# Attention 1 of a four-part layer stack: the causal mask applied to the probabilities by GpSimd instead of to the scores by TensorE

## The chip, the cores and the metric

The kernel runs on one core of a Trainium2 chip. The metric is the device time of one execution in microseconds (us); the median of three runs before the change is 2347.13 us, with 2340.8 and 2350.67 us as the lowest and the highest.

## The reference

A sequence of 2 x 1024 tokens of width 128 goes through four layers: a hybrid attention with a state-space branch (attention 0, not causal), a mixture of experts, a latent attention (attention 1, causal), and a second mixture of experts. The change touches attention 1 alone:

```python
q_lat = einsum('bhtd,hdl->bhtl', q, k_eff)
attn = einsum('bhtl,bsl->bhts', q_lat, c_kv) / sqrt(hs)
attn = where(triu(ones((T, T), bool), k=1), -inf, attn)
attn = softmax(attn, axis=-1)
ctx = einsum('bhts,bsl->bhtl', attn, c_kv)
```

A query at position t must get nothing from keys behind it: their scores are minus infinity, so their probabilities are zero. There are 16 heads of width 8.

## The kernel before

`attention` (line 276) is called for both attentions; only the call of `latent_attention` (line 1877) is causal. It works in `UNITS` = 8 units, one for each group of four heads and each half of the batch. A unit has two passes that are interleaved on the engines.

The **max pass** computes scores with the queries on the partitions (`max_unit`, line 469: a score product of each 512 keys, then on the diagonal tile a product of the identity with `mask_qk` that adds -1e30 where the key lies behind the query). VectorE takes the maximum of each row (`take_max`, line 677), splits the negated maxima into three bf16 parts (`combine`, line 683), TensorE turns them (`turn_max`), ScalarE copies them to `mrow` (`rows`, line 610), and SyncE sends them by DMA into rows 96 to 98 of `qa` (`rows`, line 412), so that the second score product subtracts the maximum.

The **exp pass** has the keys on the partitions. It goes through `NE` = 24 slots (`exp_units`, line 321): 8 for the first 512 queries (query block 0, key tiles 0 to 3, two pairs of heads each) and 16 for the second 512 (key tiles 0 to 7). `MID` = 8 is the first slot of query block 1. In a slot `exp_unit` (line 501) computes the scores of two heads, `c0` being the first query that a key tile reaches, so a slot on the diagonal is 512, 384, 256 or 128 queries wide. Where key tile and query block meet on the diagonal (`kt // 4 == qb`: slots 0 to 7 and 16 to 23), each of the two products is followed by a second one of the identity with `mask_kq` (line 517). ScalarE takes the exponential of each head into one of four buffers `probs` (line 630, f32). `pv_quad` (line 521) multiplies the probabilities of two neighbouring slots with the values; it is done in two parts, in odd slot s for slots s-3 and s-2.

What sets the order: each engine runs its own list, in order, and waits on semaphores. TensorE's list is `body` (line 560): in slot s first, if s is odd, part 0 of the product with the values, then score products of the max pass that a planner has put there in proportion to their columns (`places`, lines 336 to 347), then `exp_unit(s)`, more of the max pass, then part 1. `exp_unit` waits until ScalarE has emptied the score bank (slot s-1); ScalarE waits until the values' product of slot s-4 is done. SyncE's list (lines 438 to 445) puts, for unit i, the copies `mirror(i+1)`, then the 18 loads of unit i+2 (`load`, allowed once all scores of unit i-1 are done, that is at the start of unit i), then `rows(i, 1)`, whose arrival `exp_unit` awaits at slot `MID`, then `rows(i+1, 0)`. The last two units have no loads to make. GpSimd does nothing in these 8 units: its list (line 448) holds the preparation only, with the casts of `ident_b`, `mask_kq` and `mask_qk` (lines 453 to 456) and clearing of `ka`.

The two lines of the products with the values that matter here:

```python
if part == 0:
    pe.wait_ge(probs_ready, 2 * (NE * i + kt_slot + 2))
```

Of the kernel before, what the change touches and what calls it, by code (L numbers as in the profile page):

```python
# [6 lines left out]
BF16 = mybir.dt.bfloat16  # L7
I32 = mybir.dt.int32
ALU = mybir.AluOpType
# [6 lines left out]
BLK = 512  # L16
NBLK = T // BLK
TILE = 128
# [108 lines left out]
def sl(i, w=BLK):  # L127
    return slice(i * w, (i + 1) * w)
# [147 lines left out]
def attention(k, tag, q_lin, k_lin, k_heads, v_aug, causal, attn_t, front=None):  # L276
# [5 lines left out]
    nc = k.nc  # L282
# [5 lines left out]
    KROWS = MROW + 3  # L288
    QT = SEQ // TILE
    UNITS = 2 * GROUPS  # L290
    CONSTS = 3 if causal else 1
    RING = 3
    with ExitStack() as ctx:
        qa = [k.sb(f"{tag}_qa{i}", [KROWS, 4, SEQ], BF16, ctx) for i in range(RING)]
        ka = [k.sb(f"{tag}_ka{i}", [KROWS, nk, SEQ], BF16, ctx) for i in range(RING)]
        qu = [k.sb(f"{tag}_qu{i}", [128, 4, SEQ], BF16, ctx) for i in range(2)]
        ku = [k.sb(f"{tag}_ku{i}", [128, nk, BLK], BF16, ctx) for i in range(2)]
        probs = [k.sb(f"{tag}_probs{i}", [128, 2, BLK], F32, ctx) for i in range(4)]
# [6 lines left out]
        rden = k.sb(f"{tag}_rden", [128, 4, 4], F32, ctx)  # L305
        attn_tok = k.sb(f"{tag}_tok", [128, NT, HEADS * HD], F32, ctx)
        ident_b = k.sb(f"{tag}_identb", [128, 128], BF16, ctx)
        mask_kq = k.sb(f"{tag}_maskkq", [128, 128], BF16, ctx)
        mask_qk = k.sb(f"{tag}_maskqk", [128, 128], BF16, ctx)
        scores_max = [p.rearrange("p h t -> p (h t)") for p in k.pair[0:2]]  # L310
        scores_exp = [k.bank[4], k.bank[5]]
# [9 lines left out]
        exp_units = []  # L321
        for qb in range(2):
            for kt in range(QT if not causal else 4 * (qb + 1)):
                c0 = max(0, kt * TILE - qb * BLK) if causal else 0
                for hp in range(2):
                    exp_units.append((qb, kt, hp, c0))
        NM, NE = len(max_units), len(exp_units)
        half_end = [max(s for s, u in enumerate(exp_units) if u[0] == qb) for qb in range(2)]


# [3 lines left out]
        MID = half_end[0] + 1  # L334
        DUE = MID - 6 if not causal else MID - 5
        cost = [n + 70 for _, _, n in max_units]
        own_from = min(n for n in range(NM + 1) if sum(cost[n:]) * NE <= sum(cost) * (DUE + 1))
        stream = [(0, n) for n in range(own_from, NM)] + [(1, n) for n in range(own_from)]
        places, done, spent = [], 0, 0
        for place in range(2 * NE):  # L340
# [5 lines left out]
            done = upto  # L346
# [11 lines left out]
        const_ready = k.sem(f"{tag}_const")  # L358
# [7 lines left out]
        mrow_sent = [k.sem(f"{tag}_mrow_sent{h}") for h in range(2)]  # L366
        exp_scored = k.sem(f"{tag}_exp_scored")
        probs_ready = k.sem(f"{tag}_probs_ready")
        pv_done = k.sem(f"{tag}_pv_done")
        osb_ready = k.sem(f"{tag}_osb_ready")  # L370
        oturned = k.sem(f"{tag}_oturned")
# [16 lines left out]
        with nc.Block() as block:  # L388
# [58 lines left out]
            @block.gpsimd  # L447
            def _(pool):
                nc.gpsimd.memset(ka[0][64:96, :, :], 0.0).then_inc(k_cleared[0], 1)
                pool.wait_ge(k_cleared[0], 2)  # L450
                if front:
                    front.gpsimd_first(pool)
                nc.gpsimd.tensor_copy(ident_b[:, :], k.m("ident")).then_inc(const_ready, 1)
                if causal:
                    nc.gpsimd.tensor_copy(mask_kq[:, :], k.m("mask_kq")).then_inc(const_ready, 1)
                    nc.gpsimd.tensor_copy(mask_qk[:, :], k.m("mask_qk")).then_inc(const_ready, 1)
                pool.wait_ge(const_ready, CONSTS)
                for i in range(1, RING):
                    nc.gpsimd.memset(ka[i][64:96, :, :], 0.0).then_inc(k_cleared[i], 1)
                    pool.wait_ge(k_cleared[i], 2)  # L460
                if front:
                    front.gpsimd_second(pool)

            @block.tensor
            def _(pe):
                def kj(j):
                    return 0 if shared else j
# [33 lines left out]
                def exp_unit(i, s):  # L501
                    qb, kt, hp, c0 = exp_units[s]
                    if s == 0:
                        pe.wait_ge(mrow_sent[0], 48 * (i + 1))
                    if s == MID:
                        pe.wait_ge(mrow_sent[1], 48 * (i + 1))
                    for jj in range(2):
                        if i > 0 or s > 0:
                            pe.wait_ge(probs_ready, 2 * (NE * i + s) + jj - 1)
                        j = 2 * hp + jj  # L510
                        out = scores_exp[jj]
                        diag = causal and kt // 4 == qb
                        ins = nc.tensor.matmul(out[:, c0:BLK], ka[i % RING][:, kj(j), sl(kt, TILE)],  # L513
                                               qa[i % RING][:, j, qb * BLK + c0:(qb + 1) * BLK], start=True,
                                               stop=not diag)
                        if diag:
                            ins = nc.tensor.matmul(out[:, c0:c0 + TILE], ident_b[:, :], mask_kq[:, :],
                                                   start=False, stop=True)
                        ins.then_inc(exp_scored, 1)

                def pv_quad(i, kt_slot, vstage, part):

                    qb, kt, _, c0 = exp_units[kt_slot]
                    if part == 0:
                        pe.wait_ge(probs_ready, 2 * (NE * i + kt_slot + 2))
                        if kt_slot == 0:
                            pe.wait_ge(vstaged, i + 1)
                        if kt_slot == 0 or kt_slot == MID:
                            pe.wait_ge(osb_ready, 2 * i + qb)
                    mid = (c0 + BLK) // 2  # L530
                    cols = slice(c0, mid) if part == 0 else slice(mid, BLK)
                    for j in range(4):
                        last = nc.tensor.matmul(out_acc[32 * j:32 * j + 32, cols], vstage[:, kt, kj(j), :],  # L533
                                                probs[(kt_slot + j // 2) % 4][:, j % 2, cols],

                                                start=kt == 0 and part == 0,
                                                stop=kt_slot + 1 == half_end[qb], skip_group_check=True)
                    if part == 1:
                        last.then_inc(pv_done, 2)
# [20 lines left out]
                def body(i):  # L560
                    for s in range(NE):
                        odd = s % 2 == 1
                        if odd and s > 1:
                            products_with_v = (i, s - 3, vst[i % 2])
                        elif odd and i > 0:
                            products_with_v = (i - 1, NE - 2, vst[1 - i % 2])
                        else:
                            products_with_v = None
                        if products_with_v:
                            pv_quad(*products_with_v, 0)  # L570
                        first_pass(i, 2 * s)
                        exp_unit(i, s)
                        if s == done_half[1] + 2:
                            turn_max(i, 1)
                        if s == done_half[0] + 2 and i + 1 < UNITS:
                            turn_max(i + 1, 0)
                        first_pass(i, 2 * s + 1)
                        if products_with_v:
                            pv_quad(*products_with_v, 1)
                        if s == 3 and i > 0:  # L580
                            turn_out(i - 1, 1)
                        if s == MID + 3:
                            turn_out(i, 0)

                if front:
                    front.tensor_first(pe)
                pe.wait_ge(const_ready, CONSTS)
                for n in range(own_from):
# [7 lines left out]
                for part in range(2):  # L596
                    pv_quad(UNITS - 1, NE - 2, vst[1], part)
# [617 lines left out]
def hybrid_attention(k, d, x_in, consts_in, rest_in, hc, rall, attn_t):  # L1215

    with ExitStack() as ctx:
        v_aug = k.sb("v_aug", [128, NT, KV, 32], ctx=ctx)
        work = [buf[:, sl(b)] for buf in (attn_t, k.hn) for b in blocks(T)]
        work += [k.sb(f"front_work{i}", [128, BLK], ctx=ctx)[:, :] for i in range(2)]  # L1220
        front = HybridFront(k, d, ctx, x_in, consts_in, rest_in, hc, rall, v_aug, work)
        attention(k, "attn0", by_head(d["q_lin"]), by_head(d["k_lin"][:, 0:32]), KV, v_aug, False, attn_t, front)
# [603 lines left out]
def latent_attention(k, d):  # L1826

    nc = k.nc
    with ExitStack() as ctx:
# [12 lines left out]
        with ExitStack() as pre:  # L1842
# [32 lines left out]
            split3(k, "split_q1", [(qf, parts, tmp, send_linear(k, d["q_lin"], parts))], T)  # L1875
            split3(k, "split_k1", [(kf, parts, tmp, send_linear(k, d["k_lin"], parts))], T)
        attention(k, "attn1", by_head(d["q_lin"]), by_head(d["k_lin"]), HEADS, v_aug, True, attn_t)
        with nc.Block() as block:
            @block.vector
# [691 lines left out]
```

## Time and profile before

| What | Value |
|---|---|
| median of 3 runs | 2347.13 us |
| the profiled execution's own time | 2365.25 us |
| its span in the profile | 2363.4 us |
| TensorE busy, share of the span | 1855.2 us, 78% |
| VectorE busy | 1590.9 us, 67% |
| ScalarE busy | 1403.2 us, 59% |
| GpSimd busy | 647.2 us, 27% |
| mean granted TensorE clock | 0.836 of full speed |

Line numbers (L517) are those of the kernel before. "banks" are the PSUM banks; attn_probs, attn_qa, attn_ka, attn_mrow are the buffers named above. PE is TensorE, PEld its weight load, DVE VectorE, ACT ScalarE, POOL GpSimd, SPq the queue of SyncE. A matmul's end is modelled, so distances from one start to the next say more than durations. "[x <-y]" in a timeline is the engine's idle time before the instruction and what ended it. An f32 product with the values stands in the timeline as two instructions for each of the four heads (x8).

### The profile page before, as it was taken

To read this page: it belongs to the slowest core of one execution; us is meant where nothing else is said; L and a number is where in the kernel's file an instruction comes from. 1 tells how busy PE (TensorE), PEld (TensorE's weight loads), DVE (VectorE), ACT (ScalarE), POOL (GpSimd) and SP (SyncE) were. 2 spreads that over 40 slices of the span, in tenths; PEclk is the share of its full clock that TensorE was granted. 3 is DMA by queue.
4 is the path that set the end of the run, shared out by engine and by line. 5 is a ranking of instruction groups with operands and counts; after the bars stand their busy time and mean duration, and the time that the engine had idled before them with its cause. 6 is when DMAs were issued, how large, how long until landed. Compare 5 with 4: busy or idle time off the path is not lost. (4 is left out here: it accounts for less than half of the span.)

```text
span 2363.4 us, 31926 instructions
## 1 busy us (share of the span) xinstructions
PE 1855.2 (78%) x10382; PEld 767.3 (32%) x10382; DVE 1590.9 (67%) x1569; ACT 1403.2 (59%) x2909; POOL 647.2 (27%) x347
## 2 busy tenths in 40 slices
PE   6899999963766666776776778739998995999994
PEld 1233333322333332333333433413333334333331
DVE  6788888533999998899999231366555533466463
ACT  2477777724999996999998122305555462453432
POOL 1000000000888888788888001010000000000000
PEclk8799999986788877777767779659898896799996
DMA  3211210002655553665554010043222100000000
GB/s 141 53 24 27 43 26 12 2 0 63 214 205 195 194 191 122 206 211 189 194 194 143 1 72 0 29 96 52 35 48 44 27 2 15 0 0 0 0 5 13
DMA packets 56819, 182.31 MB, mean 77 GB/s; under 512 B 8357, under 2 KB 11712, under 8 KB 55040
## 3 DMA queue, kind: packets, MB, share of 16 engines
q1 hardware_dynamic: 56056, 179.74, 24.9%
q10 hardware_dynamic: 648, 1.04, 0.2%
q8 instruction: 71, 1.16, 0.2%
q14 instruction: 44, 0.36, 0.1%
HBM read 160.56 MB, written 7.21 MB: 71 GB/s over the span
## 5 line engine op out<-in xcount | busy, mean ns | idle before, releaser
L1585 POOL TENSOR_TENSOR hc<-st,ct 128x1024 f32<-128x1024 f32 x256 | 599.2, 2361 | 102.5 <-DVE st L1564 102.5
L680 DVE TENSOR_REDUCE attn_mx<-banks 128x1 f32<-128x1024 f32 (+7 forms) x512 | 502.2, 990 | 177.8 <-PE banks L485 120.9
L630 ACT ACTIVATE attn_probs<-banks 128x512 f32<-128x512 f32 (+3 forms) x896 | 446.2, 550 | 278.1 <-PE banks L513 177.6
L1564 DVE TENSOR_TENSOR_SCAN st<-da,banks 128x1024 f32<-128x1024 f32 x256 | 568.6, 2271 | 28.6 <-ACT da L1525 21.6
L1533 ACT ACTIVATE ut<-b_turned,x_now 128x128 f32<-128x128 f32 x1280 | 389.4, 387 | 1.7
L1453 PE MATMUL banks<-mats,ut 128*128 128x128 f32 x1280 | 251.4, 344 | 96.7 <-DVE st L1564 74.6
L1525 ACT ACTIVATE da<-dt,a_now 128x1024 f32<-128x1024 f32 x256 | 286.9, 1139 | 21.5 <-DVE st L1564 13.5
L513 PE MATMUL banks<-attn_qa,attn_ka 99*128 99x512 bf16 (+3 forms) x896 | 274.6, 376 | 19.8 <-DMA attn_qa<-attn_mrow 17.9
L533 PE MATMUL banks<-attn_probs,attn_vst 128*32 128x256 f32 (+3 forms) x3584 | 273.7, 377 | 4.1 <-ACT attn_osb L621 3.8
L1453 PEld LDWEIGHTS banks<-mats,ut 128*128 128x128 f32 x1280 | 190.4, 169 | 234.3 <-ACT ut L1533 144.7
L483 PE MATMUL banks<-attn_ka,attn_qa 64*128 64x512 bf16 (+3 forms) x512 | 203.1, 397 | 74.0 <-DMA attn_ku<-attn_ka 52.2
L1469 PE MATMUL banks<-hc,onecol 128*32 128x512 f32 x1024 | 189.1, 822 | 65.9 <-POOL onecol L1583 53.0
L2167 PE MATMUL banks<-hid_m,ew 128*128 128x512 f32 x320 | 150.2, 613 | 0.0
L483 PE MATMUL banks<-attn_ku,attn_qu 64*128 64x512 bf16 (+3 forms) x384 | 145.7, 380 | 0.0
L513 PEld LDWEIGHTS banks<-attn_qa,attn_ka 99*128 99x128 bf16 x896 | 80.9, 98 | 146.9 <-ACT attn_probs L630 55.3
L483 PEld LDWEIGHTS banks<-attn_ka,attn_qa 64*128 64x128 bf16 x512 | 47.9, 94 | 246.6 <-issue 174.4
L1460 PE MATMUL banks<-xparts,sel 96*128 96x512 bf16 x192 | 73.1, 470 | 57.4 <-DVE st L1564 56.8
L1279 POOL MEMSET onehot<- 128x1024 bf16 x1 | 1.0, 956 | 421.9 <-SPq L1265 421.9
L1558 DVE TENSOR_TENSOR banks<-bt,banks 128x1024 f32<-128x1024 f32 x96 | 115.9, 1207 | 0.0
L533 PEld LDWEIGHTS banks<-attn_probs,attn_vst 128*32 128x32 f32 x3584 | 73.7, 109 | 102.9 <-issue 91.9
L2343 DVE TENSOR_TENSOR beta<-beta,beta_raw 128x1536 f32<-128x1536 f32 x8 | 14.1, 1758 | 106.0 <-ACT beta L2273 106.0
L2167 PEld LDWEIGHTS banks<-hid_m,ew 128*128 128x128 f32 x320 | 58.3, 192 | 70.5 <-issue 70.5
(409 smaller groups left out, 1829.4 us busy)
## 6 DMA issues: line engine op xcount, KB each, us to landing
dt<-dt_rows SPq DMA_DIRECT2D x256, 512.0 KB, 4.1
attn_qa<-q_lin SPq DMA_DIRECT2D x144, 64.0 KB
attn_qu<-attn_qa SPq DMA_DIRECT2D x16, 512.0 KB, 4.2
moe_w<-in_moe_w SPq DMA_DIRECT2D x2, 2048.0 KB, 9.9
attn_ka<-k_lin SPq DMA_DIRECT2D x63, 64.0 KB
mats<-in_mats SPq DMA_DIRECT2D x1, 2844.5 KB, 15.1
attn_ku<-attn_ka SPq DMA_DIRECT2D x8, 256.0 KB, 5.0
q_lin<-qparts SPq DMA_DIRECT2D x6, 256.0 KB
```

Of the source, the lines that this page charges most:

```text
L483: ins = nc.tensor.matmul(out[:, lo:hi], lhs, rhs, start=True, stop=not diag)
L513: ins = nc.tensor.matmul(out[:, c0:BLK], ka[i % RING][:, kj(j), sl(kt, TILE)], qa[i % RING][:, j, qb * BLK + c0:(qb + 1) * BLK], start=Tru ...
L533: last = nc.tensor.matmul(out_acc[32 * j:32 * j + 32, cols], vstage[:, kt, kj(j), :], probs[(kt_slot + j // 2) % 4][:, j % 2, cols],  star ...
L630: nc.scalar.activation(probs[s % 4][:, jj, c0:BLK], scores_exp[jj][:, c0:BLK], ACT.Exp, scale=scale).then_inc(probs_ready, 1)
L680: nc.vector.reduce_max(mx[:, qt, j:j + 1], scores_max[n % 2][:, 0:w], AX.X)\
L1453: ins = nc.tensor.transpose(pair[:, i // 4, sl(i % 4, TILE)], buf[:, i, :], k.m("ident"))
L1469: last = nc.tensor.matmul(y_bank[h][32 * g:32 * g + 32, :], col[jp % 2][:, :], hc[(4 * jp + g) % 8][:, sl(h)], start=False, stop=False, sk ...
L1525: nc.scalar.activation(da[n % 4][:, :], dt[n % 4][:, :], ACT.Exp, scale=a_now[:, g, jp:jp + 1])\
L1533: nc.scalar.activation(ut[TURNED.index(n) % 2][:, i, :], b_turned[:, 8 * b + i, :], ACT.Copy, scale=x_now[:, i, g, jp:jp + 1]).then_inc(ut ...
L1564: nc.vector.tensor_tensor_scan(st[n % 4][:, :], da[n % 4][:, :], pair[:, :, :].rearrange("p h t -> p (h t)"), 0.0, ALU.mult, ALU.add).then ...
L1585: nc.gpsimd.tensor_tensor(hc[n % 8][:, :], st[n % 4][:, :], ct[:, b * SEQ:(b + 1) * SEQ], ALU.mult)\
L2167: last = nc.tensor.matmul(out[:, :], w2[:, p, comp * D:(comp + 1) * D], hid_m[u % 2][:, s, p, :], start=False, stop=p == PAIRS - 1)
```

## The change

GpSimd gets a loop. For each of the 16 diagonal slots of a unit it waits until both exponentials of the slot are written, and sets to zero, in place, every element of the 128 x 2 x 128 diagonal tile whose key (partition) lies behind its query (column), by position. TensorE's product of identity and `mask_kq` falls away, as do `mask_kq` and its cast. Part 0 of the products with the values waits in addition for both selects of its two slots. The mask of the max pass stays.

```diff
-    CONSTS = 3 if causal else 1
+    CONSTS = 2 if causal else 1
...
-        mask_kq = k.sb(f"{tag}_maskkq", [128, 128], BF16, ctx)
...
+        DIAGONAL = [s for s, (qb, kt, _, _) in enumerate(exp_units) if causal and kt // 4 == qb]
...
+        probs_cut = k.sem(f"{tag}_probs_cut")
...
-                    nc.gpsimd.tensor_copy(mask_kq[:, :], k.m("mask_kq")).then_inc(const_ready, 1)
...
+                def cut(i, s):
+
+                    _, _, _, c0 = exp_units[s]
+                    done = len(DIAGONAL) * i + DIAGONAL.index(s)
+                    pool.wait_ge(probs_ready, 2 * (NE * i + s + 1))
+                    if done:
+                        pool.wait_ge(probs_cut, done)
+                    own_keys = probs[s % 4][:, :, c0:c0 + TILE]
+                    nc.gpsimd.affine_select(out=own_keys, in_=own_keys, compare_op=ALU.is_ge, fill=0.0, base=0,
+                                            pattern=[[0, 2], [1, TILE]], channel_multiplier=-1).then_inc(probs_cut, 1)
+
+                for i in range(UNITS):
+                    for s in DIAGONAL:
+                        cut(i, s)
...
-                        diag = causal and kt // 4 == qb
-                        ins = nc.tensor.matmul(out[:, c0:BLK], ka[i % RING][:, kj(j), sl(kt, TILE)],
-                                               qa[i % RING][:, j, qb * BLK + c0:(qb + 1) * BLK], start=True,
-                                               stop=not diag)
-                        if diag:
-                            ins = nc.tensor.matmul(out[:, c0:c0 + TILE], ident_b[:, :], mask_kq[:, :],
-                                                   start=False, stop=True)
-                        ins.then_inc(exp_scored, 1)
+                        nc.tensor.matmul(out[:, c0:BLK], ka[i % RING][:, kj(j), sl(kt, TILE)],
+                                         qa[i % RING][:, j, qb * BLK + c0:(qb + 1) * BLK], start=True,
+                                         stop=True).then_inc(exp_scored, 1)
...
                         pe.wait_ge(probs_ready, 2 * (NE * i + kt_slot + 2))
+                        if kt_slot in DIAGONAL:
+                            pe.wait_ge(probs_cut, len(DIAGONAL) * i + DIAGONAL.index(kt_slot) + 2)
```

## Rows read from the trace of the kernel before

**Rows 1.** Busy time by stretch: halves of units 4, 6, 7; sum of all 16 halves.

```profile
core 0: us, PE busy (x) PEld busy (x) DVE busy (x) ACT busy (x) POOL busy (x), PEclk, DMA share, GB/s
...
1774.17:1793.85 19.68, 14.33 (x141) 7.08 (x142) 10.63 (x23) 7.93 (x20) 0.00 (x0) 0.92 0.46 62
1793.85:1824.51 30.66, 30.61 (x235) 11.05 (x236) 16.26 (x24) 15.71 (x34) 0.00 (x0) 0.78 0.13 27
...
1873.68:1889.00 15.32, 14.16 (x141) 7.06 (x142) 10.08 (x22) 7.93 (x20) 0.00 (x0) 1.00 0.01 2
1889.00:1914.08 25.08, 24.96 (x238) 9.72 (x238) 16.73 (x25) 15.61 (x34) 0.00 (x0) 1.00 0.01 2
...
1926.22:1948.38 22.16, 21.48 (x200) 7.68 (x200) 0.55 (x2) 15.21 (x33) 0.00 (x0) 0.85 0.00 1
sum 353.98, PE 327.81 PEld 133.58 DVE 194.52 ACT 187.28 POOL 0.00; mean PE 20.49 PEld 8.35 DVE 12.16 ACT 11.71 POOL 0.00
```

**Rows 2.** Waits, 1590 to 1950 us: who waited for whom, total, times, longest.

```profile
PE banks L513 <- DMA attn_qa<-attn_mrow: 16.9, 7, 4.2
```

**Rows 3.** Timeline of PE: a slot with masks, then one without (start, us).

```profile
1862.63 0.39 PE L513 MATMUL banks<-attn_qa,attn_ka 99*128 99x512 bf16 x1
...
1862.85 0.22 PE L517 MATMUL banks<-attn_maskkq,attn_identb 128*128 128x128 bf16 x1
...
1862.91 0.38 PE L513 MATMUL banks<-attn_qa,attn_ka 99*128 99x512 bf16 x1
...
1863.28 0.39 PE L483 MATMUL banks<-attn_ka,attn_qa 64*128 64x512 bf16 x1
...
1899.84 0.60 PE L513 MATMUL banks<-attn_qa,attn_ka 99*128 99x512 bf16 x2
...
1900.38 0.39 PE L483 MATMUL banks<-attn_ka,attn_qa 64*128 64x512 bf16 x1
```

**Rows 4.** SyncE's timeline: the first load of unit 7, at unit 5's start.

```profile
1824.14 0.27 SPq L385 DMA_DIRECT2D attn_ka<-k_lin  x1
```

**Rows 5.** Groups of GpSimd instructions: shapes, count | busy, mean ns.

```profile
L1281 POOL TENSOR_SCALAR_AFFINE_SELECT onehot<-onehot 128x1024 bf16<-128x1024 bf16 x1 | 3.0, 3013 | 0.2 <-POOL onehot L1279 0.2
...
L889 POOL TENSOR_TENSOR hn<-attn_t,qparts 128x512 f32<-128x512 f32 x2 | 2.3, 1154 | 39.0 <-ACT qparts L1052 39.0
...
L1583 POOL CAST onecol<-onehot 128x32 f32<-128x32 bf16 x8 | 1.7, 207 | 47.5 <-POOLq L238 40.7 <-POOLq L1593 6.7
...
L453 POOL CAST attn_identb<-mats 128x128 bf16<-128x128 f32 x2 | 0.6, 290 | 3.9 <-DVE attn_ka L727 3.2 <-DMA cols<-in_cols 0.7
```

**Rows 6.** Timeline: GpSimd starts after a VectorE instruction that it awaits.

```profile
1551.41 3.47 DVE L727 MEMSET attn_ka<- 3x4096 bf16 x1 [0.91 <-issue]
...
1554.94 3.50 POOL L459 MEMSET attn_ka<- 32x4096 bf16 x1 [2.29 <-DVE attn_ka L727]
```

**Rows 7.** Timeline, units 5 and 6: second exponentials and the products that use them.

```profile
1864.88 1.09 ACT L630 ACTIVATE attn_probs<-banks 128x512 f32<-128x512 f32 x2 [0.62 <-PE banks L517]
...
1867.07 0.64 PE L533 MATMUL banks<-attn_probs,attn_vst 128*32 128x256 f32 x8
...
1868.13 0.87 ACT L630 ACTIVATE attn_probs<-banks 128x384 f32<-128x384 f32 x2 [0.73 <-PE banks L517]
...
1869.68 0.53 PE L533 MATMUL banks<-attn_probs,attn_vst 128*32 128x192 f32 x8
...
1870.96 0.66 ACT L630 ACTIVATE attn_probs<-banks 128x256 f32<-128x256 f32 x2 [0.62 <-PE banks L517]
...
1872.14 0.42 PE L533 MATMUL banks<-attn_probs,attn_vst 128*32 128x128 f32 x8
...
1873.26 0.45 ACT L630 ACTIVATE attn_probs<-banks 128x128 f32<-128x128 f32 x2 [0.63 <-PE banks L517]
...
1874.81 0.32 PE L533 MATMUL banks<-attn_probs,attn_vst 128*32 128x64 f32 x8
...
1875.61 1.08 ACT L630 ACTIVATE attn_probs<-banks 128x512 f32<-128x512 f32 x2 [0.30 <-PE banks L517]
...
1877.33 0.64 PE L533 MATMUL banks<-attn_probs,attn_vst 128*32 128x256 f32 x8 [0.19 <-ACT attn_osb L621]
```

**Rows 8.** Timeline, unit 7, slots 16 to 19: the same for the last unit.

```profile
1939.86 2.31 ACT L630 ACTIVATE attn_probs<-banks 128x512 f32<-128x512 f32 x4 [0.35 <-PE banks L517]
...
1942.55 0.64 PE L533 MATMUL banks<-attn_probs,attn_vst 128*32 128x256 f32 x8
```

## The prediction

> **What bounds the kernel now.** I read the busy time by stretch first, cutting the 8 units of attention 1 at slot 0 and at slot MID, then the waits, then the timelines of a few slots. The 16 halves cover 353.98 us of the span, TensorE is busy for 327.81 us of them, ScalarE for 187.28 and GpSimd for none [rows 1]. Everything that the change does happens in these 354 us.
>
> Two different things set the end there.
>
> The second half of a unit (slots 8 to 23) is TensorE's. At full clock it takes 25.08 us with TensorE busy for 24.96 [rows 1], and the starts in a slot follow each other without a hole: score products, max pass, values, score products again. Whatever is taken off TensorE's list here comes off the time, and whatever makes it wait is added.
>
> The first half (slots 0 to 7) of units 1 to 5 is the DMA's. In unit 6, which has no loads beside it, it takes 15.32 us; in unit 4, with the same instructions and 14.33 us of TensorE work, 19.68 us [rows 1]. The rest is a pause before slot MID for the row maxima, up to 4.2 us and seven times in all [rows 2]. The maxima lie in SyncE's queue behind 18 loads that start with the unit (1824.14 us for unit 5, which began at 1823.8) [rows 4], and no speed of TensorE in slots 0 to 7 brings their landing forward. So what is gained in the first half of units 1 to 5 becomes a longer pause. The same holds for unit 0, where the loads are issued before the unit starts (its pause is under half a microsecond). Behind each long pause the granted clock is at its lower level (1.2 GHz) for a while: the second half of unit 4 ran at 0.78 and took 30.66 us, that of unit 6 at 1.00 and took 25.08 [rows 1]. A drop costs up to 5.6 us.
>
> **Part 1: 256 mask products go.** In a slot with masks the score products start at 1862.63 and the next line at 1863.28, 0.65 us; without masks 1899.84 to 1900.38, 0.54 us [rows 3]. The mask starts at 1862.85 and the next score product 0.06 us later. So a mask costs 0.055 us of TensorE's list, not the 0.22 us that its row shows, and a slot 0.11 us. Eight diagonal slots in each half: 0.9 us off each half at full clock (they lie in slots 16 to 23, which the timelines show at full clock). ScalarE starts 0.05 us sooner after the first score product, the product with the values 0.11 us sooner per slot.
>
> The cast of mask_kq (about 0.29 us, as the 128x128 cast in [rows 5]) goes from the preparation. It is hidden: GpSimd waited 2.29 us there for VectorE's clearing [rows 6]. It is worth nothing, and would be worth at most its 0.3 us.
>
> **Part 2: 128 selects come, and a wait.** GpSimd is empty here, so its busy time is free; what counts is that a select lies between the last exponential of a pair of slots and part 0 of the product with the values. Behind that waiting product stands all of TensorE's list, so each microsecond of the wait delays the next scores, ScalarE and VectorE too.
>
> The length of the select: the trace has one, 1024 bf16 elements per partition in 3013 ns [rows 5]. A quarter of it for 256 elements is 0.75 us; with 0.15 us of it as a fixed part it is 0.15 + 256 x 2.8 ns = 0.87 us. I take 0.85. Lower bound: a cast takes 207 ns for 32 elements and 290 for 128 [rows 5], which carried on to 256 gives 0.40 us. Upper bound: 1.15 us, what GpSimd needs for 512 elements from two inputs [rows 5]. The row of the same operation is the nearest, hence 0.85.
>
> The Trainium skill speaks against this: its GPSIMD Engine Reference, section "Engine selection", calls operations with one input roughly line-rate. By it 256 elements at the 1.2 GHz of its specification table would need about 0.2 us and some fixed part, an estimate from that page. The one select in the trace, at 2.9 ns per element, does not agree.
>
> The handovers: GpSimd started at 1554.94 after a VectorE instruction that ended at 1554.88, 0.06 us [rows 6]. I put 0.09 us on the way to TensorE, between nothing and 0.2. The step between exponential and product is then 0.06 + 0.85 + 0.09 = 1.00 us.
>
> The room it finds, from the end of the second exponential to the start of the product [rows 7]:
> - slots 16, 17: 1865.97 to 1867.07, 1.10 us; less 0.17 (masks of two slots 0.22, less the 0.05 above) 0.93. Wait 0.07.
> - slots 18, 19: 1869.00 to 1869.68, 0.68, less 0.17: 0.51. Wait 0.49.
> - slots 20, 21: 1871.62 to 1872.14, 0.52, less 0.17: 0.35. Wait 0.65.
> - slots 22, 23: 1873.71 to 1874.81, 1.10: wait 0.07, in the next unit's first half.
> - slots 0, 1: 1876.69 to 1877.33, 0.64, set by ScalarE's copy of the output: wait 0.36.
> - slots 2 to 7: their products come 1.6 us and more after the exponentials; no wait.
>
> **The sum.** Second halves of units 0 to 6: 0.07 + 0.49 + 0.65 = 1.21 us of waits against 0.90 of masks, +0.31 each, +2.2 us. Unit 7 has no max pass to put between: its exponentials of slot 17 end at 1942.17 and the product starts at 1942.55 [rows 8], 0.38 us, and the three later pairs have less. Four waits of 0.7 to 0.95 us, 3.2 together, less 0.9 of masks and 0.3 of waits on ScalarE that fall together with them: +2.0 us. First halves: units 0 to 5 nothing (the pause at MID covers it; without that cover they would gain 0.4 each), units 6 and 7 together -0.5 us, since part of the gain meets a wait for VectorE near slot 4. The pause at MID grows by about 0.45 us in five units; if the lower clock lasts a little longer for it I put 0.2 us on each, +1.0. Sum: 2.2 + 2.0 - 0.5 + 1.0 = +4.7 us. Against the profiled execution's own 2365.25 us (span 2363.4) that is 2370; that execution stands 18 us above the median, so I add the difference to the median: 2347.13 + 4.7 = 2351.8 us. About 0.5% (11.7 us) is what a measurement of this kernel can tell from no change; this is 0.2%.
>
> **Rivals.**
> 1. *The select is fast.* With 0.40 us the step is 0.55 us and only slots 18 to 21 wait, 0.24 us per unit: -0.66 x 7 = -4.6, unit 7 +0.2, first halves -0.9: -5.3 us, 2341.8. For it: the trace's only select may hold a first-use share, and its pattern has 32 short rows where the new one has 2 long ones. Against it: nothing shows a select below 2.9 ns per element. Chance 0.2. (The skill's line-rate rule would lead here.)
> 2. *A first call is slow.* If GpSimd must fetch the code of the select in unit 0, the first product waits for it, and the pause at MID covers under 0.5 us. Bound: the trace's whole select, 3 us; with the waits of the forecast +8, 2355. For it: the select's kind has not run for 1000 us by then. Against it: the idle time before the earlier one was 0.2 us [rows 5]. Chance 0.05. The skill's GPSIMD Engine Reference, "Instruction dispatch", states about 6 us for a first call; by that it would be +11.
> 3. *The selects become the bound, and the clock follows.* A select of 1.15 us or more makes the step 1.3 us: waits of 2.1 us in a second half, +1.2 x 7, unit 7 +3.2, clock +1, first halves +0.3: +13 us. If the pauses in slots 19 to 23 also bring down the clock in the units that keep it now (0 and 6), up to 5.6 us each, +24, 2371. It decides from about 0.35 us more per select than I take. For it: a software engine with its own handover, twice. Against: the pauses here are now at most 1 us and did not drop the clock in unit 6. Chance 0.15.
> 4. *A drop of the clock goes away.* With fewer columns in slots 16 to 23 or another rhythm, one or two units keep full clock, -5.6 us each; with rival 1 that reaches -12 to -16, 2333. Nothing in the rows speaks for it, since the pause at MID stays. Chance 0.07.
>
> **The numbers.** The forecast (select of 0.65 to 1.05 us, 2346 to 2357) has 0.53. The range 2338 to 2364 takes in both bounds of the select with a few microseconds of spread between medians (the three runs span 10 us), and leaves out rival 4 and the far half of rival 3. Faster by over 0.5%: 0.08 (rival 4 and a little). Slower: 0.17 (rival 3 and some of the forecast's far end). Same: 0.75.
>
> **What would show it.** No L517; 128 selects of 0.85 us; in the waits of TensorE a new line for GpSimd's probs of some 10 to 14 us, in slots 19, 21 and 23 of each unit; second halves at full clock of 25.4 us where unit 6 has 25.08; a first half of unit 4 of 19.7 us as before, with a longer wait for the maxima. It is wrong if a select takes over 1.1 or under 0.6 us, if first halves with loads get shorter, or if units 0 or 6 show the lower clock.

## The result, and the profile after

The change made the kernel slower. Right after the prediction the changed kernel took 2367.16 us (median of 4 runs, 2358.6 to 2370.02) and the kernel before 2347.41 us (4 runs): ratio 1.0082, 95% interval 1.0047 to 1.0116. Two larger sets followed, 1.0049 (1.0020 to 1.0078) and 1.0057 (1.0030 to 1.0085). The three agree on some 0.6%, medians 10 to 20 us apart; forecast were +4.7 us. Medians here count every execution, ratios and their intervals leave out those more than 1.5% above the fastest of their kernel (one of 3247 us in e1 and two in f1 below).

The profiled execution after took 2358.6 us (span 2356.8), that of before 2365.25 us. The one is the lowest of its four, the other lies above all four of its kernel, so their spans say nothing about the sign. What they say is where the time lies.

Profile page, and the group of the select (L472; lines of the changed kernel are 12 to 15 higher, so L513 is L527, L533 is L545):

```profile
PE 1839.6 (78%) x10123; PEld 751.3 (32%) x10126; DVE 1591.9 (68%) x1569; ACT 1403.4 (60%) x2909; POOL 699.6 (30%) x474
...
L472 POOL TENSOR_SCALAR_AFFINE_SELECT attn_probs<-attn_probs 128x256 f32<-128x256 f32 x128 | 52.3, 409 | 338.4 <-ACT attn_probs L642 338.4
```

128 selects of 0.41 us: half of what the prediction took, and its lower bound almost exactly. In its waits TensorE hardly appears behind them:

```profile
PE banks L527 <- DMA attn_qa<-attn_mrow: 11.8, 5, 2.9
...
PE banks L545 <- POOL attn_probs L472: 2.7, 10, 0.8
```

A timeline of unit 6, slots 21 to 23, shows the whole step. ScalarE ends at 1907.93 (1907.27 + 0.66), the select starts 0.06 us later, ends at 1908.40, the product starts at 1908.55; it waited 0.21 us.

```profile
1907.27 0.66 ACT L642 ACTIVATE attn_probs<-banks 128x256 f32<-128x256 f32 x2 [0.63 <-PE banks L527]
...
1907.99 0.41 POOL L472 TENSOR_SCALAR_AFFINE_SELECT attn_probs<-attn_probs 128x256 f32<-128x256 f32 x1 [0.88 <-ACT attn_probs L642]
...
1908.55 0.43 PE L545 MATMUL banks<-attn_probs,attn_vst 128*32 128x128 f32 x8 [0.21 <-POOL attn_probs L472]
```

First both halves of unit 0 in the kernel before, then the halves of units 0, 4 and 6 after the change (columns as in [rows 1]: stretch, its length, busy time of PE, PEld, DVE, ACT, POOL, granted clock, DMA):

```profile
1594.37:1610.46 16.09, 14.66 (x118) 6.34 (x118) 10.97 (x22) 7.64 (x18) 0.00 (x0) 0.84 0.47 66
1610.46:1635.54 25.08, 24.96 (x235) 9.72 (x236) 16.31 (x25) 15.56 (x34) 0.00 (x0) 1.00 0.15 33
```

```profile
1591.64:1610.86 19.22, 18.45 (x103) 5.71 (x103) 10.65 (x21) 7.63 (x18) 3.30 (x8) 0.50 0.38 53
1610.86:1640.21 29.35, 28.98 (x220) 9.88 (x221) 16.69 (x25) 15.66 (x34) 2.86 (x7) 0.80 0.13 28
1777.08:1793.86 16.78, 13.56 (x125) 6.22 (x126) 10.91 (x23) 7.99 (x20) 3.67 (x9) 0.98 0.45 73
1793.86:1822.24 28.38, 28.01 (x220) 9.08 (x220) 16.14 (x24) 15.71 (x34) 2.86 (x7) 0.83 0.13 29
1869.05:1885.44 16.39, 15.00 (x125) 7.09 (x126) 10.29 (x22) 7.99 (x20) 3.67 (x9) 0.90 0.01 2
1885.44:1910.04 24.60, 24.16 (x221) 8.67 (x220) 16.70 (x25) 15.61 (x34) 2.86 (x7) 1.00 0.01 2
```

Against [rows 1]: the second half of unit 6 at full clock went from 25.08 to 24.60 us, a gain. Its first half went from 15.32 to 16.39 us although TensorE has less to do, and the clock there is 0.90 where it was 1.00. Unit 0 ran its first half wholly at the lower level (1.2 GHz, 0.50) and took 48.6 us, where it had taken 41.2.

### The profile page after: what moved, and what is told of

Same layout as the page of the kernel before. It is cut to its first block and busy times, and to the rows that moved or that the text cites. A ratio compares the mean times of both kernels' runs of the same rounds, so it can differ in the third digit from the quotient of the medians.

```text
span 2356.8 us, 31732 instructions
## 1 busy us (share of the span) xinstructions
PE 1839.6 (78%) x10123; PEld 751.3 (32%) x10126; DVE 1591.9 (68%) x1569; ACT 1403.4 (60%) x2909; POOL 699.6 (30%) x474
## 5 line engine op out<-in xcount | busy, mean ns | idle before, releaser
L545 PE MATMUL banks<-attn_probs,attn_vst 128*32 128x256 f32 (+3 forms) x3584 | 277.5, 381 | 8.3 <-ACT attn_osb L633 4.5
L527 PE MATMUL banks<-attn_qa,attn_ka 99*128 99x512 bf16 (+3 forms) x896 | 269.0, 378 | 15.4 <-DMA attn_qa<-attn_mrow 12.8
L472 POOL TENSOR_SCALAR_AFFINE_SELECT attn_probs<-attn_probs 128x256 f32<-128x256 f32 x128 | 52.3, 409 | 338.4 <-ACT attn_probs L642 338.4
L527 PEld LDWEIGHTS banks<-attn_qa,attn_ka 99*128 99x128 bf16 x896 | 76.2, 99 | 138.1 <-ACT attn_probs L642 55.3
L545 PEld LDWEIGHTS banks<-attn_probs,attn_vst 128*32 128x32 f32 x3584 | 74.7, 110 | 108.6 <-issue 96.8
```

## The experiments

Eighteen runs; e0 and f0 repeat the changed kernel, f1 the kernel before, k0 and k1 two of the others. Given are medians, and ratios to executions of the kernel before on the same chip.

**Undoing one part at a time.** e0 is the changed kernel again. e1 keeps the mask products beside selects and waits. e2 has neither (`cut()` falls away too), e3 runs the selects on a buffer of their own, with no wait. Both leave the mask of the second pass out of the result.

```diff
 # e2, e3 (e3 keeps cut(), on `aside`)
-                        if kt_slot in DIAGONAL:
-                            pe.wait_ge(probs_cut, len(DIAGONAL) * i + DIAGONAL.index(kt_slot) + 2)
...
-                    own_keys = probs[s % 4][:, :, c0:c0 + TILE]
+                    own_keys = aside[:, :, :]
```

> The changed kernel once more. Its profile shows selects of 0.41 us and only 2.7 us of waits of TensorE for them, so by the instructions of attention 1 alone it should be 3 to 5 us faster than before, and its median is 20 us slower. Theory A (the granted clock of attention 1 falls, because TensorE has fewer columns and a new short pause per pair of slots): ratio 1.006 to 1.010 again, and its profile shows in attention 1 drops of the clock that the kernel before does not have. Theory B (the clock in other stages, or the draw of the runs, made the difference): ratio 0.995 to 1.003 this time.

> TensorE's mask products stay and the selects with their waits come on top. Theory A with the removal of columns as the cause: back to the time of before, 0.999 to 1.003. Theory A with the pauses for GpSimd as the cause: as slow as the change, 1.006 to 1.012. Theory B: 1.000 to 1.003, the waits alone cost some 3 us.

> No mask products on the exponential pass and no selects, no waits: keys behind a query are not masked in the second pass (this part of the computation is left out). Theory A with the removal as the cause: 1.005 to 1.010, as the change. Theory A with the pauses as the cause: faster than before, 0.995 to 0.998 (0.055 us for each of the 256 masks, 14 us at most, some 8 us outside the first halves that wait for the DMA). Theory B: 0.995 to 0.998 too.

> No mask products; the 128 selects run at the same moments, but on a buffer of their own, and TensorE does not wait for them (the mask of the second pass is left out of the result). Against the run with neither it shows what the presence of the selects costs without the wait: all theories expect no difference to that run beyond 0.002; if it is slower by more, GpSimd's work itself (the port shared with VectorE, or the chip's clock) is the cause.

Measured: e0 2363.54 us, 1.0049 (1.0020 to 1.0078); e1 2361.31 us, 1.0026 (0.9996 to 1.0056); e2 2351.48 us, 0.9987 (0.9963 to 1.0012); e3 2357.06 us, 0.9999 (0.9971 to 1.0028). The interval of e0 lies above 1 again, so the draw of the runs was not the cause; the clock of other stages, the other half of theory B, is not excluded by it. Neither part alone shows the loss, and e2, which does strictly less than the kernel before, is not clearly faster. Executions of the kernel before spread over 2335 to 2372 us here, wider than the effect.

**Attention 1 six times in a row**, to multiply the effect: the call of attention in `latent_attention` goes into a loop of six with a tag each.

> The kernel before with attention 1 computed six times in a row (each time from the same data, so the result stays). It is the base for the next three; time is that of before plus five times preparation and loop of attention 1, about 5 x 400 us, so 4350 us. Its six loops give six draws of the clock. All theories: loops of 350 to 358 us, second halves of 25.1 us wherever the clock is at its upper level, and no drop of the clock within the first half of a unit.

> The changed kernel with attention 1 six times. Theory A (attention 1 itself became slower, by the granted clock): 6 x 8 to 12 us over the run with six times before, +48 to +70 us, with a mean clock in the loops that is lower, and drops of 3.4 us within first halves. Theory C (attention 1's instructions take 4 to 6 us less and the clock gives that back, no more; the rest of the 11 us of the single kernel is draw): -20 to +25 us.

> No mask products on the second pass, no selects, no waits (the mask of the second pass is left out), attention 1 six times. By the columns alone 0.9 us per second half at full clock and 8 of them: -7 us and more per loop, -40 to -55 us over six. If the removal of columns itself costs clock (short drops in first halves), it gives part of that back: theory A with that cause says -10 to +30 us, theory C -25 to -45 us.

> Masks kept, selects and waits on top, attention 1 six times. The waits alone: second halves of 25.17 us against 25.08 in the single profiles, so +1 to +3 us per loop, +6 to +20 us by the instructions. Theory A with the pauses for GpSimd as the cause: +40 to +60 us. No short drops in first halves, as in the single run with both.

Measured: r0 4447.48, r1 4454.19, r2 4422.45, r3 4460.12 us (6 runs each, each set spread over 37 to 55 us). The medians of r0 and r1 lie 7 us apart, less than either set spreads, and their intervals overlap (1.8771 to 1.8900, 1.8835 to 1.8946): the +48 to +70 us of theory A did not come, and what remains fits the -20 to +25 of theory C. The mean granted clock, however, split cleanly by one thing only: 0.839 to 0.846 and 0.834 to 0.845 in the executions of r0 and r3 (masks there), 0.820 to 0.833 and 0.823 to 0.829 in those of r1 and r2 (masks gone). So taking the mask products out lowers the granted clock. A drop is a stretch at the lower level. In the traces r0 and r3 have no drop that begins in a first half and lasts only some 3.4 us, r1 has 16 of them and r2 has 5, in 48 units each.

**Taking the noise away.** The pauses for the row maxima at slot MID and the low clock behind them fall differently in each execution. They come from SyncE's order, so the line that sends the row maxima (three small DMAs) was moved ahead of the loads, in both kernels (h0, h1). f0 and f1 are the changed kernel and the kernel before once more.

```diff
+                    rows(i, 1)
                     if i + 2 < UNITS:
                         load(i + 2)
-                    rows(i, 1)
```

> The changed kernel a third time, beside the kernel before as a labelled kernel of its own. So far it was 20 us above the kernel before (4 runs each) and 11 us (12 against 35 runs), while with attention 1 six times the difference was 5 us in all. Theory A (a real loss of about 10 us): 1.003 to 1.007 again. Theory C (attention 1 costs nothing, the rest was draw): 0.998 to 1.003.

> The kernel before against itself: 0.998 to 1.002. If it lands outside, two sets of twelve runs of one kernel differ by as much as the effect that is looked for.

> The kernel before, with one line of SyncE's list moved: the row maxima of the second half are sent before the 18 loads of unit i+2, not behind them. The pauses of 1 to 4 us at slot MID should go, and with them the 10 to 17 us at the lower clock behind each; five units of attention 1 at 5 to 9 us each give -25 to -40 us, ratio 0.983 to 0.990 (attention 0, which shares the line, may add to it). If the pauses stay or return at the unit's start, since the loads now come later: 0.997 to 1.003.

> The changed kernel with the same line moved. Without the DMA's pause nothing hides what the change does in the first halves. By instructions (0.9 us off each half, 0.4 us of waits for the selects in a second half and some in a first) it should be 6 to 9 us faster than the kernel before with the line moved, ratio to that 0.996 to 0.998. Theory A (fewer columns bring short drops of the clock): those drops now cost their full 1.4 us each in up to eight first halves, and it is no faster, or up to 5 us slower, than that kernel.

Measured: f0 2367.22 us, 1.0057 (1.0030 to 1.0085); f1 2362.34 us, 1.0008 (0.9969 to 1.0046); h0 2320.48 us, 0.9862 (0.9824 to 0.9901); h1 2334.41 us, 0.9909 (0.9880 to 0.9937). With the pauses gone the six runs of h0 lie within 2318.5 to 2325.3 us and the twelve of h1 within 2327.7 to 2340.3: no overlap, 14 us apart (2334.41 - 2320.48), and now it can be read why. Attention 0 shares the moved line, but unit 0 of attention 1 starts at 1590.92 us in f1 and at 1591.49 in h0, so what the line gives, it gives in attention 1 and behind it. First h0, both halves of unit 0, then of unit 1:

```profile
1591.49:1606.76 15.27, 14.29 (x119) 6.27 (x120) 10.55 (x21) 7.61 (x18) 0.00 (x0) 0.85 0.02 3
1606.76:1631.83 25.07, 24.95 (x236) 9.72 (x237) 16.72 (x25) 15.60 (x34) 0.00 (x0) 1.00 0.51 80
1631.83:1647.15 15.32, 14.16 (x141) 7.04 (x142) 10.07 (x22) 8.10 (x20) 0.00 (x0) 1.00 0.02 5
1647.15:1672.23 25.08, 24.96 (x238) 9.72 (x237) 16.72 (x25) 15.64 (x34) 0.00 (x0) 1.00 0.50 79
```

The same of h1:

```profile
1592.40:1611.64 19.24, 18.47 (x102) 5.70 (x103) 10.64 (x21) 7.62 (x18) 3.28 (x8) 0.50 0.07 12
1611.64:1641.12 29.48, 29.12 (x221) 9.93 (x221) 16.67 (x25) 15.65 (x34) 2.84 (x7) 0.80 0.38 61
1641.12:1657.48 16.36, 15.00 (x126) 7.08 (x126) 10.35 (x22) 8.10 (x20) 3.66 (x9) 0.90 0.01 4
1657.48:1682.06 24.58, 24.15 (x219) 8.65 (x220) 16.68 (x25) 15.60 (x34) 2.84 (x7) 1.00 0.50 82
```

The loops, from the first to the last score product of the exp pass, took 315.4 and 328.0 us, +12.6, and it adds up: unit 0 +8.4 (48.7 against 40.3, the clock at the lower level for 31 of its 49 us), first halves of units 1 to 6 +1.05 each, +6.3, their second halves -0.49 each, -2.9, unit 7 +0.8.

Where the drop in a first half falls is seen in finer stretches of h1's unit 1 (16.36 us in four parts):

```profile
1641.12:1644.50 3.38, 3.25 (x28) 1.24 (x28) 2.77 (x3) 2.87 (x7) 1.22 (x3) 1.00 0.02 7
1644.50:1648.00 3.50, 2.27 (x23) 0.83 (x23) 2.42 (x6) 2.59 (x6) 0.81 (x2) 0.94 0.00 0
1648.00:1651.00 3.00, 3.00 (x19) 2.06 (x11) 0.87 (x5) 0.00 (x0) 0.00 (x0) 0.51 0.01 3
1651.00:1657.48 6.48, 6.48 (x66) 2.96 (x65) 4.30 (x11) 2.65 (x9) 1.63 (x4) 1.00 0.01 4
```

Before it falls TensorE is busy for 2.27 of 3.5 us: it waits there for VectorE's maxima, in slot 4. h0 has that wait too (2.35 of 3.50 us) and keeps its clock:

```profile
1635.20:1638.70 3.50, 2.35 (x27) 0.96 (x25) 2.42 (x6) 2.69 (x6) 0.00 (x0) 1.00 0.00 0
```

**Which part, and which half.** The same line moved in all four: h2 without masks, selects or waits; h3 with all of them; h4 with masks in slots 0 to 7 and selects in 16 to 23; h5 the reverse (`qb == 0` in the line below). Of the two theories that follow, R is that the removal of the mask products brings the low clock, W that the waits for GpSimd bring it.

```diff
-        DIAGONAL = [s for s, (qb, kt, _, _) in enumerate(exp_units) if causal and kt // 4 == qb]
+        DIAGONAL = [s for s, (qb, kt, _, _) in enumerate(exp_units) if causal and kt // 4 == qb and qb == 1]
...
-                        diag = causal and kt // 4 == qb
+                        diag = causal and kt // 4 == qb and s not in DIAGONAL
```

> With the row maxima sent first: no mask products on the second pass, no selects, no waits (the second pass is left unmasked). Theory R (the removal of the mask columns brings the drops of 3.4 us in first halves and the longer start at the lower clock in unit 0): both are there, first halves of 16.3 us where there is a drop, second halves 24.19 us, unit 0 some 8 us longer; 2328 to 2333 us, slower than the same kernel with masks (2320) although it does less. Theory W (the waits for GpSimd bring them): no drops, 2310 to 2314 us.

> With the row maxima sent first: masks kept, selects and waits on top. Theory R: no drops, 2320 to 2323 us (0.1 us of waits per half). Theory W: drops in first halves and 2330 us or more.

> With the row maxima sent first: TensorE's masks in slots 0 to 7, GpSimd's selects with their waits only in slots 16 to 23. Theory R: it is the columns in slots 0 to 7, where TensorE also waits for VectorE, that hold the clock up; so no drops, first halves 15.3 us, second halves 24.6, -0.48 us x 7: 2316 to 2318 us, the fastest of all. If the columns of the second half matter as much: drops somewhere in second halves and 2320 us or more.

> With the row maxima sent first: the other way round, selects in slots 0 to 7, masks in slots 16 to 23. Theory R: a drop of 3.4 us in each first half and the long low clock in unit 0, second halves 25.1 us; 2335 to 2340 us, the slowest of these.

Measured: h2 2323.52 us, 0.9858 (0.9816 to 0.9900); h3 2325.97, 0.9874 (0.9831 to 0.9916); h4 2322.66, 0.9872 (0.9827 to 0.9918); h5 2329.34, 0.9892 (0.9849 to 0.9935). Only h3 and h4 came slower than theory R had it (2320 to 2323 and 2316 to 2318).

From the traces, in us (start to start of the first score product; halves of units 1 to 6 where the clock stayed up):

| Kernel | slots 0-7 | slots 16-23 | unit 0 | first half | second half | drops in first halves, units 1-6 | loop |
|---|---|---|---|---|---|---|---|
| h0 | mask | mask | 40.3 | 15.32 | 25.08 | 0 | 315.4 |
| h3 | both | both | 40.3 | 15.32 | 25.17 | 0 | 317.4 |
| h4 | mask | select | 39.9 | 15.32 | 24.58 | 0 | 312.6 |
| h5 | select | mask | 49.1 | 14.98 | 25.08 | 0 | 323.2 |
| h2 | none | none | 48.2 | 14.98 | 24.19 | 1 | 317.2 |
| h1 | select | select | 48.7 | (16.37 with drop) | 24.58 | 6 | 328.0 |

The column of unit 0 splits by slots 0 to 7 alone. Its halves in h2, which has no select at all, in h4, and in h5, whose slots 16 to 23 keep the masks:

```profile
1595.68:1613.97 18.29, 17.19 (x103) 5.53 (x104) 10.56 (x21) 7.63 (x18) 0.00 (x0) 0.59 0.07 13
1613.97:1643.88 29.91, 29.80 (x220) 10.07 (x221) 16.64 (x25) 15.65 (x34) 0.00 (x0) 0.77 0.37 60
```

```profile
1589.77:1605.09 15.32, 14.34 (x118) 6.26 (x119) 10.56 (x21) 7.63 (x18) 0.00 (x0) 0.85 0.01 3
1605.09:1629.67 24.58, 24.14 (x222) 8.65 (x221) 16.69 (x25) 15.56 (x34) 2.84 (x7) 1.00 0.49 81
```

```profile
1590.11:1609.33 19.22, 18.45 (x103) 5.71 (x104) 10.64 (x21) 7.63 (x18) 3.29 (x8) 0.50 0.06 12
1609.33:1639.16 29.83, 29.78 (x237) 10.93 (x237) 16.73 (x25) 15.66 (x34) 0.00 (x0) 0.80 0.31 60
```

Theory R holds for unit 0, and theory W falls for it. For the short drops R is half right: they need the masks of slots 0 to 7 gone (not one in any trace that has these masks, r0 and r3 included), but with them gone they came six times in h1, once in h2 and not once in h5. So the missing products alone do not tell how often they come. Nor are the six of h1 six independent events: they begin 40.96 us apart, and a unit with a drop lasts 40.95 to 40.99 us there, so each unit meets its drop at the same place, 6.4 us behind its start. The measured 2323.5 us of h2 is below the 2328 to 2333 expected since five of the expected drops, 1.4 us each, did not come. h5 was expected at 2335 to 2340 and came at 2329, with the long unit 0 but no short drops.

**Does the select pay where the masks of slots 0 to 7 stay?** h0 and h4 again, on one chip.

> The kernel before with the row maxima sent first, again, to stand on one chip beside the next one: 2318 to 2324 us, ratio 0.984 to 0.988.

> Selects in slots 16 to 23 alone, row maxima first, again. Its loop took 312.6 us in one trace against 315.4 us for the kernel with masks throughout; if the clock of unit 0 is as good as there, it is 2 to 3 us faster than k0. If in some executions unit 0 starts at the lower clock more often than in k0, it is the same or up to 5 us slower on the median, and its runs spread wider.

Measured: k0 2321.02 us, 0.9898 (0.9849 to 0.9946); k1 2321.43 us, 0.9894 (0.9845 to 0.9942). No difference, although k1's loop is 1.6 us shorter in its trace (313.0 against 314.6). Two things in the traces take that back. The loop as counted here ends before the last select is awaited; up to the end of the last product with the values it is 314.8 against 315.7 us. And what follows attention 1 is longer wherever only slots 16 to 23 have selects: 414.4 us in h4 and 415.0 in k1 from that product to the end, 409.6 to 411.8 in h0, h1, h2, h3, h5 and k0. The first 110 us of it show a lower clock, here h4 and then h0:

```profile
1904.21:2014.21 110.00, 78.44 (x276) 43.15 (x276) 48.80 (x89) 36.33 (x57) 0.00 (x0) 0.71 0.02 8
...
1908.10:2018.10 110.00, 78.54 (x284) 41.62 (x284) 48.15 (x89) 36.53 (x58) 0.00 (x0) 0.74 0.02 8
```

These 3 us and more would account for most of what h4 lacked against its forecast. Why the clock is lower there was not tried. The version to keep is the kernel before with the row maxima sent first.

## Why the prediction was wrong

The medians rose by 10 to 20 us against the +4.7 forecast, and the first median lies above the range. Step by step:

- **What bounds the halves: right.** Second halves are TensorE's, column by column. Predicted 0.9 us for the 16 masks of a half; h0 against h2 gives 25.08 - 24.19 = 0.89 us. First halves of units 1 to 5 wait for the row maxima behind the loads: moving them ahead took 26 to 36 us off, pauses and the low clock behind them together. The 0.4 us that an uncovered first half would gain is there too: 15.32 against 14.98 us where the clock stayed up.
- **The length of the select: wrong by a factor of two.** "The row of the same operation is the nearest, hence 0.85": it is 0.41 us. The 3013 ns of the old select were for 1024 elements in rows of 32, in bf16; 2.9 ns per element did not carry over to two rows of 128 in f32. Which of the two, rows or type, makes the difference was not tried. The row of the plain cast, taken as lower bound, gave 0.40. The Trainium skill's GPSIMD Engine Reference, "Engine selection", had called one-input operations roughly line-rate; 256 elements in 0.41 us lie at 1.6 ns each, fixed part included, nearer to that than to the row I trusted.
- **The waits: their mechanism right, their size too large with it.** With the step at 0.06 + 0.41 + 0.15 = 0.62 us a second half pays 24.58 - 24.19 = 0.39 us for waits, not 1.21. The prediction's own rooms give the same with that step: 0.62 - 0.51 and 0.62 - 0.35, together 0.38. By rival 1's reckoning it would have been 0.24, and by it the kernel should have been 5 us faster. By instructions a second half did gain, 0.49 us.
- **The terms for the first halves ("units 0 to 5 nothing") and for the clock (+1.0): this is the step that failed.** The clock was put down to pauses at MID and the rest of the list was held to be neutral to it. It is not. Unit 0 starts at the lower level, coming from the preparation. With the masks in slots 0 to 7 it rises 3.3 to 5.0 us into the first half and stays up there (seven traces of eight). Without them it either does not rise in the first half (after, h1, h5) or rises, falls again 3.4 us later and stays low for 24 us (e0, e2, e3, f0, h2). In the traces of the single kernels and the h and k kernels unit 0 took 39.4 to 41.2 us in seven of eight with those masks (49.2 in e1) and 48.0 to 49.1 in all eight without. The masks are not enough in every case: e1 has them together with the selects, and so has r3, whose first unit 0 took 48.4 us; h3, with both as well, took 40.3. What made the difference stays open. These are 8 us that no term of the sum held. The other part, short drops near slot 4 at about 1.4 us each (16.38 against 14.98 us), came three or four times in the loops of the changed kernel; in units 1 to 5 the pause at MID can hide them. The prediction's own sign of being wrong, the lower clock in units 0 or 6, came in both, and so did the other, a select under 0.6 us.
- **Rival 3 (slow selects, +13 us and more) gave about the right time for the wrong reason, which is luck.** Its second sentence, that the clock of unit 0 might fall, named the place, but tied it to selects of 1.15 us. Rival 2 (a slow first call) did not come: no select took over 0.44 us, and the first started 0.14 us after its exponential.

The six repetitions fit this, without testing it. There unit 0 is slow with masks too (43.9 to 48.9 us in the six calls of r0, 47.6 to 48.8 in those of r1), and the term of 8 us shrinks to 1.3 in the mean (48.28 against 46.95). In r0 all six have a drop in the second half (granted clock 0.82 to 0.88), which the single kernels with masks did not have but for e1, and three have a first half at 0.59; why is open.

The Trainium skill ("TensorE: Matmul & The Clock Gate", section on HAM oscillation) describes TensorE falling back to its slower clock through waits for DMA between bursts. The traces agree for the pauses at MID: in f1 each unit with a pause of 3 us and more has a second half of 29.6 to 30.3 us, each without 25.07. The removed masks are a different case: the waits of h0 and h1 near slot 4 are nearly equal, and only the work around them differs.

What stays open: why the short drops come six times in h1, once in h2 and never in h5; why masks beside selects kept the clock of unit 0 in h3 but not in e1 and r3; and why the clock behind attention 1 is lower in h4 and k1. Nor was it tried whether any other cheap products in slots 0 to 7 would hold the clock as the masks do; that it is the work as such is argued, not shown.

## What to carry to other kernels

Removing cheap work from TensorE can cost more than the work did, by way of its granted clock: here 256 products of 0.055 us were worth 0.9 us per half, and their absence in the first half of the first unit cost 8 us. Read the granted clock of each stage before and after, not only the busy times, and remove noise from it (here three small DMAs moved ahead of 18 loads, worth 1 to 1.4% themselves) before judging a change of half a per cent. For an operation's cost, take the row with a like access pattern and length, not only the row with the same name.

## What the runs showed of the hardware

- GpSimd's select on 128 x 256 f32 in place took 0.41 us. It started 0.06 to 0.07 us after the exponential that it awaited, and a product that waited for it started 0.15 us after its end.
- A mask product of 128 columns cost TensorE 0.055 us in its list at full clock. With these products in slots 0 to 7 unit 0 took some 40 us in seven of eight traces, without them 48 to 49 us in eight of eight.
- Small DMAs queued behind 18 loads of 64 KB made TensorE pause up to 4.3 us in these traces; each pause of 3 us and more in f1 was followed by a second half 4.5 to 5.2 us longer. With the order turned, six executions lay within 7 us where those of the kernel before spread over 38.
